# A fused attention and FP4 feed-forward kernel: the row shift of the layer norm moves to GpSimd, and three groups of small operations change their place in the queues

## The reference

```python
xn = _layernorm(x, axis=-1)                      # (x - mean) / sqrt(var + 1e-5)
x = x + _L0_attn_ref(xn, ...) + _L0_ffn_ref(xn, ...)
# attention: q = rope(xn @ Wqa @ Wqb), 16 heads of 8; k, v from xn @ Wkva @ Wkvb, 4 heads;
#            causal softmax(q k^T * scale) @ v, then @ Wout + bout
# feed-forward, every operand of a product quantised in blocks of 16 along its last axis:
def fp4_quant_dequant(x):
    scale = max(|block|) / 6, at least 1e-12
    return _GRID[searchsorted(_MID, |x / scale|)] * sign(x) * scale
h = silu(q(xn) @ q(w_gate).T) * (q(xn) @ q(w_up).T)
out = q(h) @ q(w_down).T
```

## Time and profile before

| | us |
|---|---|
| median of three runs | 790.27 |
| the profiled execution | 788.24 |
| its span from first to last instruction | 785.8 |
| PE busy | 718.4 |
| DVE busy | 627.7 |
| POOL busy | 588.6 |
| ACT busy | 535.9 |

### The profile page before, as it was taken

How to read it: one execution, slowest core, us unless ns; L and a number is a source line. 1 busy time by engine, 2 the same in 40 slices (tenths; PEclk the granted TensorE clock), 3 DMA queues, 4 the chain that set the end, 5 groups by cost and what they waited for, 6 DMA issues and landing times.

```text
span 785.8 us, 18291 instructions
## 1 busy us (share of the span) xinstructions
PE 718.4 (91%) x6453; PEld 440.8 (56%) x6453; DVE 627.7 (80%) x1424; ACT 535.9 (68%) x1154; POOL 588.6 (75%) x630
## 2 busy tenths in 40 slices
PE   2467899999999999999999999999999999999886
PEld 1233455665656565665656565665656565665443
DVE  6569888889798888989798888989798888878412
ACT  2213676867777777867777777877777777777772
POOL 4533597878879797868889797878788797856662
PEclk9999899999999999999999999999999999999999
DMA  4432224334334433344334334243334333241111
GB/s 111 108 77 82 67 76 109 93 106 113 99 93 117 103 114 97 94 106 113 97 94 119 104 109 105 89 117 104 96 99 126 94 117 95 77 115 46 57 50 49
DMA packets 84885, 75.41 MB, mean 96 GB/s; under 512 B 28627, under 2 KB 66868, under 8 KB 84796
## 3 DMA queue, kind: packets, MB, share of 16 engines
q1 hardware_dynamic: 84796, 74.25, 35.1%
HBM read 40.38 MB, written 27.25 MB: 86 GB/s over the span
## 4 chain that ended last, share of the span: by engine, by line
PE 62%; DVE 15%; ACT 7%; POOL 6%; issue 4%; DMA 3%; SPq 2%; POOLq 0%; DVEq 0%; ACTq 0%
PE pv_ps L1159 16%; PE exp_ps L1137 12%; PE max_ps L1122 8%; DVE neg_max L732 7%; PE misc_ps L1183 5%; PE max_ps L1123 5%; PE misc_ps L1220 5%; ACT P L958 3%; PE misc_ps L1191 3%; PE misc_ps L1208 3%; PE misc_ps L1218 2%; POOL P L555 2%; PE misc_ps L1169 1%; DVE h_mag L694 1%; PE misc_ps L1187 1%
## 5 line engine op out<-in xcount | busy, mean ns | idle before, releaser
L732 DVE TENSOR_REDUCE neg_max<-max_ps 128x1 f32<-128x512 f32 (+3 forms) x768 | 430.4, 593 | 88.2 <-PE max_ps L1123 86.1
L958 ACT ACTIVATE P<-exp_ps 128x512 f32<-128x512 f32 x512 | 294.7, 599 | 164.0 <-PE exp_ps L1137 163.0
L1137 PE MATMUL exp_ps<-Q,K 128*128 128x512 bf16 (+3 forms) x1024 | 243.4, 301 | 10.2 <-ACT P L958 6.8
L1122 PE MATMUL max_ps<-K,Q 128*128 128x384 bf16 (+2 forms) x768 | 198.9, 278 | 20.1 <-DMA Kd<-K 10.5
L1123 PE MATMUL max_ps<-Kd,Q 128*128 128x128 bf16 x1024 | 190.7, 220 | 1.4 <-DVE neg_max L732 1.2
L555 POOL TENSOR_SCALAR_AFFINE_SELECT P<-P 128x512 f32<-128x512 f32 x256 | 161.7, 667 | 30.6 <-ACT P L961 30.6
L1159 PE MATMUL pv_ps<-P,V 128*32 128x512 f32 (+3 forms) x2048 | 163.9, 438 | 1.2 <-POOL P L555 0.8
L1122 PEld LDWEIGHTS max_ps<-K,Q 128*128 128x128 bf16 x768 | 75.6, 99 | 97.6 <-DVE neg_max L732 53.8
L1123 PEld LDWEIGHTS max_ps<-Kd,Q 128*128 128x128 bf16 x1024 | 99.0, 100 | 42.5 <-issue 22.7
L1137 PEld LDWEIGHTS exp_ps<-Q,K 128*128 128x128 bf16 x1024 | 79.6, 98 | 48.0 <-ACT P L958 26.4
L586 POOL TENSOR_TENSOR h<-gate_sb,up_half 128x352 f32<-128x352 f32 x64 | 59.5, 930 | 54.6 <-DVE gate_sb L745 54.5
(11 more groups left out here) (126 smaller groups left out, 962.7 us busy)
## 6 DMA issues: line engine op xcount, KB each, us to landing
Q<-q_scr SPq DMA_DIRECT2D x64, 224.0 KB
o_scr<-oT SPq DMA_DIRECT2D x31, 256.0 KB, 3.3
q_scr<-q_split SPq DMA_DIRECT2D x16, 384.0 KB, 2.6
Kd<-K SPq DMA_DIRECT2D x64, 96.0 KB
x_in<-x SPq DMA_DIRECT2D x16, 256.0 KB, 4.7
q_scr<-q_split SPq DMA_DIRECT2D x16, 256.0 KB, 2.9
x_res<-x SPq DMA_DIRECT2D x16, 256.0 KB, 5.7
out<-y SPq DMA_DIRECT2D x32, 128.0 KB, 4.4
```

The lines of the kernel that those rows point to most:

```text
L732: nc.vector.tensor_reduce(neg_max[:, pr // 4, heads[0]:heads[0] + len(heads), pr % 4, i], max_ps[r % 3][:, 0:len(heads) * n].rearrange("p ...
L958: nc.scalar.activation(P[g % 2][:, hh + r % 2, col:col + 512], ps[:, :], ACT.Exp, scale=SCALE).then_inc(exp_done, 1)
L1122: nc.tensor.matmul(ps[:, col:col + d], Qt, Kt[:, half, g, 0:d], start=True, stop=True)
L1137: last = nc.tensor.matmul(exp_ps[n % 2][:, col:col + width], K[par][:, half, pr // 2, kb * 128:(kb + 1) * 128], Q[par][:, pr, kb * 128:S], ...
```

## The change

There are three parts.

1. The shift is computed on POOL, as a `tensor_tensor` product right behind `rstd`. For that DVE makes `neg_mean` = -mean with a `tensor_scalar` beside `var_eps`, and DVE's own product at the start of slot 5 goes. `var_done` now counts two a batch. `bn_aggr` stands behind the third maximum tile of slot 3 and the two `tensor_scalar` behind the fourth, each one tile earlier than before.
2. Two of the four `bn_stats`, with the wait for `x_loaded`, stand at the end of slot 1. The other two stay in slot 3.
3. ACT's copy for the magnitudes of x stands behind the third exponential tile of slot 0, DVE's two instructions on it behind the sixth maximum tile.

```diff
@@ POOL, deviation
-                T.wait(pool, var_done, 1, 3, 1)
+                T.wait(pool, var_done, 2, 3, 2)
                 nc.gpsimd.tensor_tensor(rstd[:, :], var_eps[:, :], half_neg[:, :], ALU.pow).then_inc(rstd_done, 1)
+                T.wait(pool, rstd_done, 2, 3, 1)
+                nc.gpsimd.tensor_tensor(shift[:, :], neg_mean[:, :], rstd[:, :], ALU.mult).then_inc(rstd_done, 1)
@@ DVE, slot 0
                 reduces(0, 4)
+                reduces(0, 5)
                 if T.has(2):
                     T.wait(dve, x_powers, 1, 2, 1)
                     magnitudes(lambda s, n: T.wait(dve, s, 2, 2, n), x_mag[:, :], x_mags)
-                reduces(0, 5)
@@ DVE, slot 1
                 reduces(1, 5)
+                if T.has(3):
+                    T.wait(dve, x_loaded, 16, 3, 16)
+                    for c in range(2):
+                        nc.vector.bn_stats(bn_raw[:, c, :], x_in[:, c, :]).then_inc(bn_done, 1)
@@ DVE, slot 3
                 if T.has(3):
-                    T.wait(dve, x_loaded, 16, 3, 16)
-                    for c in range(NT):
+                    for c in range(2, NT):
                         nc.vector.bn_stats(bn_raw[:, c, :], x_in[:, c, :]).then_inc(bn_done, 1)
                 reduces(3, 2)
                 gated(T, 2)
-                reduces(3, 3)
                 if T.has(3):
                     ... (four bn_aggr)
-                reduces(3, 4)
+                reduces(3, 3)
                 if T.has(3):
                     T.wait(dve, mv_done, NT, 3, NT)
                     T.wait(dve, rstd_done, 2, 2, 1)
+                    T.wait(dve, rstd_done, 2, 2, 2)
+                    nc.vector.tensor_scalar(neg_mean[:, :], bn_mv[:, :, 0], -1.0, None, ALU.mult).then_inc(var_done, 1)
                     nc.vector.tensor_scalar(var_eps[:, :], bn_mv[:, :, 1], EPS, None, ALU.add).then_inc(var_done, 1)
+                reduces(3, 4)
                 reduces(3, 5)
@@ DVE, before slot 5
-                if T.has(3):
-                    T.wait(dve, rstd_done, 2, 3, 1)
-                    nc.vector.scalar_tensor_tensor(shift[:, :], bn_mv[:, :, 0], -1.0, rstd[:, :],
-                                                   ALU.mult, ALU.mult).then_inc(rstd_done, 1)
@@ ACT, extra
-                if (slot, r) == (0, 0) and T.has(2):
+                if (slot, r) == (0, 2) and T.has(2):
                     T.wait(act, x_scaled, 1, 2, 1)
```

More of the change, by code:

```diff
@@ L173, in build @@
         rstd = sb("rstd", [128, NT])
+        neg_mean = sb("neg_mean", [128, NT])
         shift = sb("shift", [128, NT])
```

## The result

The changed kernel takes 793.68 us, the median of six runs (790.97 to 795.48). Six runs of the kernel before, beside it, have a median of 789.68 us. The ratio is 1.0046 with a 95% interval of 1.0031 to 1.0062: 3.6 us slower, with 2.4 to 4.9 us as the interval (the two medians lie 4.0 us apart). Forecast were 5.2 us more and 795.5 us.

The account below looks back on a forecast made before the run. PE's own queue was taken to set slots 0 to 3 of a full step, POOL's queue the rest up to hqT0; 6.3 - 0.3 - 0.8 = +5.2 us gave 795.5 us on the median of 790.27, range 791.5 to 799.5.

Parts of the forecast that it names:

- The start: Step -2: the moved wait for x_loaded holds q_sin and the chain to the first maximum tile, +6.3 us once.
- Rival B: First steps: the start isn't delayed, as the load lands earlier or the chain has slack; 789.5 us, chance 0.04.
- ACT's magnitudes: Slot 0: x magnitudes behind the third exponential free the PSUM bank for line 1187 earlier, -0.29 us a step.
- Rival D: Slots 0 and 1: ACT's moved magnitudes delay the next exponentials, giving slot 0's win back; 799.3 us, chance 0.1.
- POOL's shift: Between rstd and m_split, inside POOL's run that sets the step: the new product costs +0.25 us a step.
- Rival C: POOL's shift costs as much as rstd, so a step loses 0.7 us; 805 us in all, chance 0.05.
- DVE's shift goes: Slot 5: PE wins about 0.3 us but waits longer for POOL at hqT0, so 0 for the step.
- `neg_mean` and the earlier scalars: DVE's scalars one tile earlier: DVE can lose up to 0.9 us; cost taken as 0, other bound 0.1.
- A full step: Steps 0 to 12: -0.29 + 0.25 = -0.04 us each, 13 of them -0.5 us.
- Step 13: It has the x magnitudes but no layer norm: -0.3 us.
- Step -1: Later magnitudes find POOL's hidden nearly over and lose less to it: about -0.3 us.
- The halfway case: An outcome between the forecast and a rival where full steps win more and pay for the start; around 792.5 us, chance 0.1.

Follow-up runs that it names:

- the early load: Changed kernel with SP's load of x_in for batch 1 issued before the mask tables, at about 13 us instead of 25: 0.9962, 3.0 us faster than before.
- the old order in step -2: Changed kernel, but in step -2 alone the four bn_stats and the wait for x_loaded stay behind the weights: 0.9971, 2.3 us faster than before.
- Part 1 alone: Kernel before with only the shift on POOL, neg_mean and the earlier aggregates: 1.0041, 3.2 us slower.
- part 2 alone: Kernel before with only two of the four bn_stats and the wait for x_loaded moved to the end of slot 1: 1.0073, 5.8 us slower.
- the early power: Changed kernel, old order in step -2; from step -1 statistics in slots 1 and 2, POOL's power and product behind k_rope: 0.9886, 9.0 us faster than before.
- two products: Changed kernel with POOL's product of neg_mean and rstd made twice, the first into a spare tile: 1.0064 against the kernel before.

## Why the prediction was right

The forecast was slower by 5.2 us, and it is 3.6 us. By its own steps:

- **The start**, +6.3 us: the mechanism held link by link, with 5.8 to 5.9 us (`q_sin` +5.81, first maximum tile +5.92; alone 1.0073, 5.8 us). Two `bn_stats` take 0.4 us, as assumed; the difference is that SP issued the load 0.67 us earlier in the profiled execution. The prediction took the 25.51 us of one execution as fixed, and its bound of at least 5.9 us with it. The traces have the issue at 24.84 to 26.56 us. The experiment with the early load shows that it is the load; the one with the old order in step -2 that nothing else of the change costs anything there. Rival B is out.
- **ACT's magnitudes**, -0.29 us a step: -0.33 measured alone. Rival D is out. The term was sized by PE's distance of starts. The chain's 0.34 us, taken as the outer bound, was the better figure.
- **POOL's shift**, +0.25 us a step: 0.25 in POOL's own rows, 0.28 a step alone. Rival C (1.0 us) is out: the product takes 0.20 us, `rstd` 1.01.
- **DVE's shift goes**, 0 for the step, its win swallowed at `hqT0`, whose wait was to grow from 0.25 to about 0.8 us: it is 0.77. Part 1 alone shows the loss that this leaves. One detail was misread: the stop of 0.23 us at 375.08 was not DVE's shift, since it is still there (0.24 us) with the shift on POOL. PE's win in slot 5 came one maximum tile earlier, where the tile at 374.67 had come 0.26 us behind its turn and its successor of now (379.89) follows after 0.22 us.
- **`neg_mean` and the earlier scalars**, 0: DVE stood still beside a POOL instruction, as foreseen, and no PE wait hangs on it. `neg_mean` took 0.51 us here and ended at 372.05 us, with POOL's product that runs until 372.03; in step -2, at 38.94 us, where POOL was idle, it took 0.17. `var_eps` took 0.16:

```profile
371.09 0.94 POOL L587 TENSOR_TENSOR h<-gate_sb,up_half 128x352 f32<-128x352 f32 x1
```

```profile
371.54 0.51 DVE L885 TENSOR_SCALAR neg_mean<-bn_mv 128x4 f32<-128x4 f32 x1
371.96 0.16 DVE L886 TENSOR_SCALAR var_eps<-bn_mv 128x4 f32<-128x4 f32 x1
```

- **A full step**, -0.04 us: -0.09 measured. Over 13 steps that is 1.2 us instead of 0.5. Step 13, -0.3 us: -0.35 (42.64 against 42.99 us between the loads).
- **Step -1**, -0.3 us: wrong in the profiled execution, where it lost about 1 us, and by the clock. Between 66 and 69 us the granted clock was 0.50, the lower of TensorE's two levels, and four gate and up matmuls took 2.67 us, where at the same place of the kernel with part 2 alone they took 1.45. The row of the window, and the matmuls of the one and the other kernel:

```profile
66.00:69.00 3.00, 2.87 (x6) 1.45 (x7) 2.27 (x7) 1.00 (x2) 1.56 (x2) 0.50 0.00 0
```

```profile
66.74 2.67 PE L1187 MATMUL misc_ps<-wguT,xqT 128*128 128x352 f32 x4
```

```profile
66.56 1.45 PE L1186 MATMUL misc_ps<-wguT,xqT 128*128 128x352 f32 x4 [0.33 <-DVE k_sin L859]
```

Before it PE had been waiting for DVE again and again (seven times between 55 us and this stretch, 2.2 us together). From the first maximum tile to the first matmul on `m_split`, late in step -1, it was 29.97 us before and 31.11 here, which accounts for about 1 us of the 5.7 between the two profiled executions. It doesn't come in every execution. The versions with the early load and with the early power have the low clock there too (31.27 and 32.31 us). The version with two products has the same order in that step and a granted clock of 1.00 there: 29.41 us. With the old order in step -2 it is 29.83. Without the low clock, then, the stretch was 0.1 to 0.6 us shorter than before, as the -0.3 us had it.

In the profiled executions the 5.7 us add up so, read at the loads for `hqT0`: +5.92 to the first maximum tile, +1.01 from there to `hqT0` of step 0, -1.75 over the steps 1 to 12 (some 0.6 of it because two steps of before were slow), -0.35 in step 13, and +0.86 in the steps behind it. The prediction had nothing for the last of these and the wrong sign for the second. They are nearly made up by the third, so part of the closeness of 5.2 to 5.7 is luck.

By the terms as measured alone, 5.8 + 3.2 - 4.4 gives +4.6 us; the whole, measured, has +3.6 us with an interval of 2.4 to 4.9. They agree within their intervals. Of the chances 0.7 stood on a loss of more than 0.5%, 3.95 us, and the ratio gives 3.6, which is 0.3 us under that line. The halfway case, which I had given a tenth, was near.

## What to carry to other kernels

Before a wait is moved up in an in-order queue, look at it in the first steps of a pipeline and not only in a full one: here the load was in time in every full step and late in step -2, and that one wait cost more than 13 better steps brought. An engine that is busy 98% of a step isn't thereby the one that sets it; follow back from each of its small stops whether the releasing engine had any idle time since it was last released. Work taken from a queue with slack and put into an uninterrupted run of another engine arrives in the step one to one, and the same work put into an idle time of that engine ahead of the run costs only what it delays the run's start, here 0.5 of 1.25 us.

## What the runs showed that I had not expected

Steps of equal work differ, mostly by some tenths of a us, for a reason that the traces don't tie to the change. In step 14 the changed kernel lost 0.4 us in slot 0. DVE's `o_inv` waits there for the DMA that gathers the sums, before and after:

```profile
695.63 0.35 DVE L763 RECIPROCAL o_inv<-o_sum 128x32 f32<-128x32 f32 x1 [1.70 <-DMA o_sum<-o_scr]
```

```profile
700.89 0.35 DVE L766 RECIPROCAL o_inv<-o_sum 128x32 f32<-128x32 f32 x1 [2.13 <-DMA o_sum<-o_scr]
```

The wait is 0.43 us longer, and the reductions behind it and the next maximum tiles come later by as much. It can be far more: in the execution of part 1 alone one full step took 45.88 us instead of 44.23, and there DVE came to the same line at 234.47 us, after 1.91 us of waiting for this DMA. In the version with the early power the same line waited 21 times for 33.6 us together, against 11 times and 21.8 us before: this DMA is probably what is late next, once POOL's run is shorter. That was read in the profiles and not tested.
